# A Mamba block beside a mixture of experts: a quarter of the norm on GpSimd, halves in the routing, zeros spread over the loop, and a new table of units

## The reference

```
xn = (x - mean(x)) / sqrt(var(x) + eps)              # rows of 256

# Mamba: 512 channels, 16 states
x_in, z  = split(xn @ W_in)
u        = silu(causal_conv4(x_in) + conv_b)
dt, B, C = split(u @ W_xproj)                        # 16 + 16 + 16
delta    = softplus(dt @ W_dt + b_dt)
h[t]     = exp(delta[t] * A) * h[t-1] + delta[t] * u[t] * B[t]
y[t]     = sum over the 16 states of h[t] * C[t]
mamba    = ((y + D_skip * u) * silu(z)) @ W_out

# experts: 16 of them, the best 2 of each row
probs    = softmax(xn @ Wr + br); w, idx = top2(probs); w = w / sum(w)
o_e      = gelu(layernorm(xn @ W1[e] + b1[e]) * g1[e] + be1[e]) @ W2[e] + b2[e]
out      = x + mamba + sum over idx of w * o_e
```

## Time and profile before

| | |
|---|---|
| median of three runs | 1133.63 us |
| the profiled execution | 1137.55 us |
| its span, first to last instruction | 1135.8 us |
| mean granted TensorE clock | 0.902 of full speed |
| VectorE busy | 1045.8 us (92%) |
| TensorE busy | 940.2 us (83%) |
| GpSimd busy | 871.0 us (77%) |
| ScalarE busy | 864.9 us (76%) |
| DMA, mean over the span | 164 GB/s |

### The profile page before, as it was taken

How to read it: one execution, slowest core, us unless ns; L and a number is a source line. 1 busy time by engine, 2 the same in 40 slices (tenths; PEclk the granted TensorE clock), 3 DMA queues, 4 the chain that set the end, 5 groups by cost and what they waited for, 6 DMA issues and landing times.

```text
span 1135.8 us, 16904 instructions
## 1 busy us (share of the span) xinstructions
PE 940.2 (83%) x4570; PEld 639.2 (56%) x4571; DVE 1045.8 (92%) x1308; ACT 864.9 (76%) x1839; POOL 871.0 (77%) x562
## 2 busy tenths in 40 slices
PE   4927776497998999779998999899988999887865
PEld 3414343363566656556666766576656666666544
DVE  7887999999999988968998989999999999999894
ACT  4544698556698799857999689978998799976971
POOL 5057899699778788756878767977987887887894
PEclk9957887589889999879997999899997999889989
DMA  9576457973376424825447652873457543855313
GB/s 305 188 271 241 137 183 225 316 291 83 112 245 204 107 69 122 312 82 112 103 104 233 210 107 67 255 235 57 107 151 249 133 116 87 291 169 108 70 19 65
DMA packets 119367, 185.86 MB, mean 164 GB/s; under 512 B 12012, under 2 KB 104344, under 8 KB 111016
## 3 DMA queue, kind: packets, MB, share of 16 engines
q1 hardware_dynamic: 87120, 144.60, 37.7%
q0 software_dynamic: 19584, 25.26, 13.0%
q10 hardware_dynamic: 12568, 14.93, 4.3%
HBM read 146.34 MB, written 42.60 MB: 166 GB/s over the span
## 4 chain that ended last, share of the span: by engine, by line
PE 36%; DVE 18%; issue 16%; ACT 14%; POOL 9%; DMA 4%; ACTq 2%; SPq 1%; POOLq 0%; DVEq 0%
DVE hb L1555 10%; PE psY L1087 8%; POOL hc L624 5%; PE psA L1112 4%; PE psC L1225 4%; PE psA L1160 3%; ACT hb L798 3%; PE psE L1202 3%; PE psC L1175 3%; PE psA L1104 2%; DVE psB L1544 2%; ACT hnT L913 2%; PE psA L1148 2%; DMA xg<-xs_d 1%; POOL xs_d L638 1%
## 5 line engine op out<-in xcount | busy, mean ns | idle before, releaser
L624 POOL TENSOR_TENSOR hc<-hb,Cb 128x1024 f32<-128x1024 f32 x245 | 621.2, 2640 | 108.2 <-PE psY L1087 65.4
L1555 DVE TENSOR_TENSOR_SCAN hb<-hb,carry,psB 128x512 f32<-128x512 f32 x384 | 470.9, 1261 | 6.8 <-ACT hb L798 5.0
L798 ACT ACTIVATE hb<-delta,aneg 128x512 f32<-128x512 f32 x512 | 351.9, 716 | 27.5 <-POOL hc L624 21.0
L1087 PE MATMUL psY<-ident,hc 128*128 128x128 f32 x2048 | 308.0, 292 | 71.1 <-POOL hc L624 70.8
L1087 PEld LDWEIGHTS psY<-ident,hc 128*128 128x128 f32 x2048 | 258.1, 151 | 183.8 <-POOL hc L624 94.1
L1544 DVE TENSOR_TENSOR psB<-Bb,psU 128x512 f32<-128x512 f32 x512 | 324.6, 678 | 3.2 <-DMA Bb<-bc_d 3.2
L672 POOL DMA_INDIRECT out<-yo,idx x80 | 128.8, 1610 | 56.8 <-DMA out<-yo,idx 16.9
L1555 DVE TENSOR_TENSOR_SCAN hb<-hb,psB 128x512 f32<-128x512 f32 x128 | 149.3, 1202 | 0.0
L1112 PE MATMUL psA<-ux,dgw 128*128 128x512 f32 x232 | 114.0, 607 | 1.6 <-ACT ux L739 1.4
L1225 PE MATMUL psC<-w2r,hnT 128*128 128x256 f32 x320 | 89.8, 429 | 0.0
L631 POOL TENSOR_TENSOR du<-delta,ux 128x512 f32<-128x512 f32 x32 | 47.2, 1474 | 53.9 <-DVE delta L1377 51.8
(11 more groups left out here) (233 smaller groups left out, 1198.2 us busy)
## 6 DMA issues: line engine op xcount, KB each, us to landing
Bb<-bc_d SPq DMA_DIRECT2D x32, 1024.0 KB, 7.1
Cb<-bc_d SPq DMA_DIRECT2D x32, 1024.0 KB, 7.4
w1r<-w1c_d SPq DMA_DIRECT2D x80, 256.0 KB
w2r<-in_L_ffn_W SPq DMA_DIRECT2D x80, 256.0 KB, 3.4
xg<-xs_d SPq DMA_DIRECT2D x20, 516.0 KB
xg<-xn_d SPq DMA_DIRECT2D x37, 128.0 KB, 2.8
Bb<-in_L_attn_x SPq DMA_DIRECT2D x8, 512.0 KB, 8.2
xn_d<-hb SPq DMA_DIRECT2D x8, 512.0 KB, 7.9
```

The lines of the kernel that those rows point to most:

```text
L624: pool.tensor_tensor(hc[:, k:k + 2, :], hb[:, g % HR:g % HR + 2, :], Cb[:, n:n + 2, :], ALU.mult).then_inc(s_g, 1)
L798: act.activation(hb[:, g % HR, :], delta[:, dc, :], ACT.Exp, scale=aneg[:, dc, n:n + 1]).then_inc(s_exp, 1)
L1087: mm = pe.matmul(y[:, tt * P:(tt + 1) * P], hc[:, g % GR, tt * P:(tt + 1) * P], ident[:, :], start=False, stop=(n == NS - 1), is_transpose ...
L1555: dve.tensor_tensor_scan(h, h, psB[g % 2][:, :], first, ALU.mult, ALU.add).then_inc(s_scan, 1)
```

## The change

1. **Norm.** VectorE norms three of a chunk's four tiles of rows; GpSimd norms the last one (`norm_tile`), with two conv weights behind each from the second chunk on. A semaphore of its own, `s_xnp`, counts GpSimd's tiles; SyncE, TensorE, ScalarE and VectorE's statistics wait for it too.
2. **Routing.** The one-hot steps are done for the left 256 columns and then for the right 256. The first half waits for the first half of the logits only.
3. **Zeros.** Eight of the 16 zero DMAs stand ahead of the loop, the others one at each of units 0 to 7.
4. **Loads.** B's and C's second quarter of the first chunk is issued right behind the first, ahead of the row loads.
5. **Pairs.** `HC_DVE` loses 204, 274 and 416 and gains 64, 330 and 418. It has 11 pairs as before; the last is 418, so none lies in the last chunk (448 to 511).
6. **Last chunk.** Its output steps move forward by one to three units, and so its add stands at unit 61 instead of 63.
7. **Units.** Many numbers of the tables move by one to three, in `AT0` by up to nine.

```diff
-INIT_AT = 58
-ETAB_AT = 40
+INIT_AT = 57
+ETAB_AT = 38
@@ AT
-    "xd_mm": [39, 41, 41, 44],
+    "xd_mm": [41, 41, 42, 43],
-    "du": [53, 0, 25, 26],
+    "du": [53, 0, 23, 26],
...
@@ AT0
-    "d0_exp": [4, 6, 6],
-    "d0_max": [7, 8, 8],
+    "d0_exp": [3, 6, 7],
+    "d0_max": [3, 4, 5],
...
@@ AT7
-    "p_copy": [58, 58, 61, 62],
+    "p_copy": [57, 58, 59, 60],
...
-HC_DVE = [2, 10, 12, 20, 54, 56, 86, 180, 204, 274, 416]
+HC_DVE = [2, 10, 12, 20, 54, 56, 64, 86, 180, 330, 418]
+ZERO0 = 8
+ZERO_STEP = 1
@@ MOE
-    "idx": [6],
+    "idx": [4],
-    "t2": [11, 20],
+    "t2": [12, 20],
+def zero_unit(k):
+
+    return (k - ZERO0) * ZERO_STEP
+        def norm_tile(eng, g, tt):
+
+            eng.wait_ge(s_rs, g + 1)
+            if g >= NKN:
+                eng.wait_ge(s_xst[g - NKN], 16)
+                eng.wait_ge(s_tp, 2 * (g - NKN) + 2)
+            eng.tensor_scalar(xnb[g][:, tt, :], xraw[g][:, tt, :], mv[:, g % 2, tt, 0:1],
+                              rstd[:, g % 2, tt:tt + 1], ALU.subtract, ALU.mult).then_inc(s_xnp if tt == TT - 1 else s_xn, 1)
@@ sync
             load_bc(0, 0)
+            load_bc(0, 1)
             sp.wait_ge(s_w["bst"], 16 * 6)
             sp.wait_ge(s_route, 1)
             for j in range(NPLACE):
                 load_rows(j)
-            for q in range(1, NS // NQ):
+            for q in range(2, NS // NQ):
                 load_bc(0, q)
@@ gpsimd
             pool.wait_ge(s_w["conv"], 32)
-            for dc in range(DC):
-                conv_weights(dc)
+            for g in range(NC):
+                norm_tile(pool, g, TT - 1)
+                if g >= 1 and g - 1 < 2 * DC - 2:
+                    conv_weights((g - 1) // 2, (g - 1) % 2)
+            for h in range(2):
+                conv_weights(DC - 1, h)
...
             for k in range(NPAD):
-                put_zeros(k)
+                if zero_unit(k) < 0:
+                    put_zeros(k)
...
+                        for k in range(NPAD):
+                            if zero_unit(k) == G:
+                                put_zeros(k)
@@ scalar
-            act.wait_ge(s_rtd, 1)
+            act.wait_ge(s_rtd, 2)
             act.activation(scratch[7], scratch[6], ACT.Exp).then_inc(s_rte, 1)
@@ tensor
-                    pe.wait_ge(s_xn, (g + 1) * TT)
+                    pe.wait_ge(s_xn, (g + 1) * (TT - 1))
+                    pe.wait_ge(s_xnp, g + 1)
@@ vector
             def row_norm(g):
-                ...
-                for tt in range(TT):
-                    dve.tensor_scalar(xnb[g][:, tt, :], ...)
+                for tt in range(TT - 1):
+                    norm_tile(dve, g, tt)
-            dve.wait_ge(s_lg, 2)
-            onehot(lg, s32(0), s32(1), oh1, row[0], row[1])
-            dve.tensor_tensor(ie(row[6]), ie(lg), over_e(s32(0)), ALU.subtract).then_inc(s_rtd, 1)
-            link(dve.tensor_scalar(row[3], oh1, -2 * BIG, BIG, ALU.mult, ALU.add))
-            link(dve.tensor_tensor(row[4], lg, row[3], ALU.min))
-            onehot(row[4], s32(2), s32(3), oh2, row[0], row[1])
+            for h in range(2):
+                part = slice(h * T // 2, (h + 1) * T // 2)
+                dve.wait_ge(s_lg, h + 1)
+                top = onehot(h, lg, s32(0), s32(1), oh1, row[0], row[1])
+                dve.tensor_tensor(ie(row[6][:, part]), ie(lg[:, part]), top, ALU.subtract).then_inc(s_rtd, 1)
+                link(dve.tensor_scalar(row[3][:, part], oh1[:, part], -2 * BIG, BIG, ALU.mult, ALU.add))
+                link(dve.tensor_tensor(row[4][:, part], lg[:, part], row[3][:, part], ALU.min))
+                onehot(h, row[4], s32(2), s32(3), oh2, row[0], row[1])
             dve.tensor_tensor(Mb, oh1, oh2, ALU.add).then_inc(s_rtd, 1)
```

More of the change, by code:

```diff
@@ L598, in constants, with conv_weights @@
                 pool.iota(padrow[:, :], pattern=[[0, 1]], base=1 + NT, channel_multiplier=1, **kw).then_inc(s_const, 1)
-            def conv_weights(dc):
-                for k in range(KW):
+            def conv_weights(dc, h):
+                for k in range(h * KW // 2, (h + 1) * KW // 2):
                     pool.tensor_scalar(dgw[:, dc, k, :], ident[:, :], cw[:, dc, k:k + 1], None, ALU.mult).then_inc(s_wc, 1)
@@ L1459, in _, with onehot, over_half @@
-            oh1, oh2 = row[2], row[5]
-            onehot(lg, s32(0), s32(1), oh1, row[0], row[1])
-            dve.tensor_tensor(ie(row[6]), ie(lg), over_e(s32(0)), ALU.subtract).then_inc(s_rtd, 1)
-            link(dve.tensor_scalar(row[3], oh1, -2 * BIG, BIG, ALU.mult, ALU.add))
-            link(dve.tensor_tensor(row[4], lg, row[3], ALU.min))
-            onehot(row[4], s32(2), s32(3), oh2, row[0], row[1])
+            def onehot(h, src, top, first, oh, t0, t1):
+                part = slice(h * T // 2, (h + 1) * T // 2)
+                half = slice(h * TILES // 2, (h + 1) * TILES // 2)
+                def over_half(ap):
+                    return ap[:, half].unsqueeze(2).to_broadcast([P, TILES // 2, E])
+                link(dve.tensor_reduce(top[:, half], ie(src[:, part]), AX.X, ALU.max))
+                link(dve.tensor_tensor(ie(t0[:, part]), ie(src[:, part]), over_half(top), ALU.is_equal))
+                link(dve.tensor_tensor(t1[:, part], t0[:, part], iotaE[:, part], ALU.mult))
+                link(dve.tensor_reduce(first[:, half], ie(t1[:, part]), AX.X, ALU.min))
+                link(dve.tensor_tensor(ie(oh[:, part]), ie(iotaE[:, part]), over_half(first), ALU.is_equal))
+                return over_half(top)
```

95 lines of the change are left out of this document (45 added, 50 removed).

## The result

The changed kernel took 1127.53 us (median of 20 runs) beside 1131.57 for the kernel before: ratio 0.9963, 95% interval 0.9945 to 0.9981, some 4 us faster. Run again unchanged in two later sets it came to 0.9999 (0.9976 to 1.0022) and 0.9988 (0.9969 to 1.0008); weighted by their runs the three give 0.998, some 2 us. The forecast, 1121.4 from 1133.63, was a ratio of 0.989. So the size was three to five times too large; the sign is clear of the scatter in the first set alone.

The account below looks back on a forecast made before the run. VectorE, busy 1045.8 of 1135.8 us, was taken to set the pace, with TensorE close behind in the middle. Terms -5.0 - 4.5 - 1.0 + 1.0 - 2.7 = -12.2 us gave 1121.4 from the median 1133.63; range 1109 to 1131.

Parts of the forecast that it names:

- Pair 204: VectorE's 12.74 us wait at this pair's times-C goes, TensorE catching up part: -4.5 us, bounds 0 and -12.7.
- The signs named: Expected trace marks, among them smaller waits of 5 to 8 us replacing the 12.7 us wait, with TensorE busy over 95%.
- The second rival: TensorE keeps the middle: pairs 204 and 274 give nothing, half the start is taken back: -5.2, 1128.4 us; 15%.
- Pair 274: VectorE's 3.89 us wait at this pair goes in part: -1.0 us, bounds 0 and -3.9.
- End: Last chunk's add stands ahead of GpSimd's last times-C and starts sooner: -2.7 us, bounds 0 and -3.9.
- Prologue and first units: Norm, routing halves and spread zeros bring GpSimd's times-C of pair 14 sooner: -5.0 us, bounds -1.7 and -9.
- +1.0 taken back: In the middle chunks TensorE can't wholly follow an earlier VectorE: +1.0 of the 5.0 us, bounds 0 and +2.5.
- Other units: Units moved by one to three shift consumers or sources behind TensorE's and ScalarE's waits: 0, bounds +3 and -3.
- wrong if: VectorE's idle falls under 6 us, new pairs 64, 330 or 418 wait over 3 us, or clock leaves 0.88 to 0.93.
- Third rival: More TensorE pauses in middle chunks lower its granted clock; at 0.85 five chunks cost 22 us: slower, 1143 us; 8%.
- Fourth: GpSimd's norm quarters lock the shared ports and stop VectorE: +7.0 instead of -2.0, sum -3.2, 1130.4 us; 5%.

Follow-up runs that it names:

- after_oldlist: The changed kernel with VectorE's pairs of the kernel before (204, 274, 416 in place of 64, 330, 418): 1135.90 us, ratio 1.0055 to the kernel before.
- before_start: The changed kernel with all tables of units and pairs of the kernel before, leaving the start's edits: 1128.04 us, ratio 0.9973 to the kernel before.
- start_510: The start's edits alone, all tables of the kernel before, plus pair 510 on VectorE: 1126.88 us, ratio 0.9978 to the kernel before.
- after_third: The changed kernel, unchanged, timed in a third set: 1126.85 us, ratio 0.9988 to the kernel before.
- after_oldat0: The changed kernel with the whole of chunk 0's table of the kernel before: 1124.83 us, ratio 0.9939 to the kernel before.

## Why the prediction was wrong, step by step

The forecast's sum was -12.2 us, the first set measured -4.0 and the three together some -2. The start and what is taken back of it (-5.0 and +1.0) make -4.0 alone; the terms of the pairs and of the end, 8.2 us, didn't come.

- **Pair 204, -4.5: the step that failed.** The text said that TensorE is late next and "doesn't shrink", and then let half of the 9.0 us that it idles in the following 102 us be caught up. It measured 0 (1.0007). Of the idle time 7.0 us lie behind 551 us, where the gate has already taken VectorE's lead; before it TensorE works 46 of 48 us, and ScalarE's own list lets the gate go. The signs named 5 to 8 us of smaller waits in its place: between 500 and 620 us VectorE waits 14.3 us now, and waited 15.1 before. The second rival, "TensorE keeps the middle", had this step right. That its 1128.4 (15% of the chance) is near the 1129.4 that the first ratio makes of 1133.63 is in part luck, since it also took 2.7 us at the end and half of the start; all three sets together make 1131.
- **Pair 274, -1.0.** Worth nothing of its own either: from unit 272 to 288 the three profiles of after win 0.7 or 0.8 us, and the one of after_oldlist, where the pair is back with its wait of 3.6 us, wins 0.7 too.
- **End, -2.7: the other term that failed.** +0.3 in the kernel after (16.9 in the mean against 16.6), -1.6 in two kernels with the same end. I let the add start 0.3 us ahead of the last scan's end, and in the kernel after it started 1.6 behind it, held by the output's last copy, which the forecast leaves out; the last times-C then was 2.5 us late instead of 1. And I let TensorE's last matmuls keep their speed; where the add was in time, these at half speed, and not the load of the sum, ended the kernel.
- **Prologue and first units, -5.0, and +1.0 taken back.** Together -4.0; measured -4.2, -4.4 and -5.2 at unit 80. That the number fits is luck, for the path is not mine: 9 to 10 us were won by unit 64 (the bound of -9 was VectorE's, and was reached), and 5 given back at one gate. before_start, without that gate's wait, was 8.7 us ahead at unit 80 and came out at 3.1. Of the parts: the first product at 67.61 (67.2), the one-hot chain from 35.37 to 46.75 (34.6 to 46.4).
- **Other units, 0,** bounds +3 and -3. As a whole it may hold (start_510 beside after_third). Chunk 0's table costs 3 to 4 us at unit 80 by after_oldat0, in nine traces of ten, at or over the bound of +3; I had looked at none of the retimed units for a new wait. What the pad indices' new wait costs isn't shown.
- **The tests named.** Of "wrong if": VectorE's idle total fell by 8.4 us, all of it span, no new pair waited over 1.21 us, the clock was 0.915. All three spoke for the forecast in the profiled pair of runs, because the profile of before was 6 us above its own median. One profile of each was too little for a change of 1%.
- **Third rival** (slower by the clock): the clock rose, from 0.902 to 0.915. **Fourth** (the ports as a lock): see below; for the norm it didn't come, elsewhere it is there.

## What to carry to other kernels

A long wait of the bounding engine is worth only the idle time that its releaser has before the next point where the two meet. Read the releaser's busy share in exactly that stretch, not in a hundred microseconds around it: 46 of 48 us said 0. And a gain at one place is worth nothing until it has passed the next gate: the start's 9 to 10 us at unit 64 were 4 to 5 at unit 80 in the kernel after, and before_start's 8.7 at unit 80 were 3.1 in the time.
